# Order of TensorE work in a cross-attention batch: weighing directly behind the second half of the scores, and one wait of the output moved behind the fourth block's first scores

## What is computed

```python
x = x + _L0_xattn_ref(_layernorm(x), ctx_1024, Wq, Wk, Wv, Wp, bp)   # cross attention, 1601 context rows per batch
x = x + _L0_attn_ref(_layernorm(x), ...)                             # self attention over the 64 tokens, with a bias
x = x + _L0_ffn_ref(_layernorm(x), W_fc, W_proj)                     # 512 -> 2048 -> 512, then five spike steps

def _L0_xattn_ref(x, y, Wq, Wk, Wv, Wp, bp):
    q = _split_heads(x @ Wq)
    k = _split_heads(y @ Wk)
    v = _split_heads(y @ Wv)
    attn = jnp.einsum('bhid,bhjd->bhij', q, k) * SCALE
    attn = jax.nn.softmax(attn, axis=-1)
    out = jnp.einsum('bhij,bhjd->bhid', attn, v)
    ...
    return out @ Wp + bp
```

## Time and profile before

| | us |
|---|---|
| three runs | 2047.29, 2052.15, 2051.09 (median 2051.09) |
| the profiled execution, as a whole | 2046.93 |
| its span, first to last instruction | 2045.1 |
| PE busy in the span | 1890.7 (92%) |
| DVE, POOL, ACT busy | 1260.8, 909.0, 867.8 |

### The profile page before, as it was taken

The page is one execution under the profiler, slowest core; times in us unless marked ns, Lnnn a source line. Parts: engine busy times, 40 slices in busy tenths (PEclk is TensorE's granted clock), DMA queues, the critical chain, the costliest instruction groups (busy, mean ns, idle before and its releaser), DMA issues. The chain is left out here.

```text
span 2045.1 us, 65858 instructions
## 1 busy us (share of the span) xinstructions
PE 1890.7 (92%) x28992; PEld 1625.4 (79%) x28992; DVE 1260.8 (62%) x1514; ACT 867.8 (42%) x1078; POOL 909.0 (44%) x856
## 2 busy tenths in 40 slices
PE   6999999999999999999999999999997964699774
PEld 3988888888989888888889898888886853578664
DVE  4466584848475665748484756657474435642888
ACT  3444453545354444535453544445342313234341
POOL 0284453627272644536272726445363013434562
PEclk9999999999999999999999999999999985799887
DMA  5201120202020101201010201011013010222331
GB/s 198 79 4 32 43 72 3 72 3 71 3 72 3 71 29 45 72 3 72 3 71 3 72 3 71 28 47 72 2 64 111 4 32 2 78 73 103 113 123 53
DMA packets 42254, 106.09 MB, mean 52 GB/s; under 512 B 18944, under 2 KB 18944, under 8 KB 41984
## 3 DMA queue, kind: packets, MB, share of 16 engines
q1 hardware_dynamic: 41984, 101.79, 14.0%
HBM read 95.62 MB, written 6.16 MB: 50 GB/s over the span
## 5 line engine op out<-in xcount | busy, mean ns | idle before, releaser
L356 POOL TENSOR_TENSOR fold<-fold,prob 128x256 f32<-128x256 f32 (+1 forms) x704 | 673.1, 956 | 55.2
L76 PE MATMUL ring<-y_parts,wk_s 128*128 128x402 f32 (+1 forms) x3072 | 609.2, 351 | 3.7 <-PEq L129 3.7
L76 PE MATMUL ring<-wv_s,y_parts 128*128 128x512 f32 (+1 forms) x2496 | 598.3, 397 | 0.0
L76 PEld LDWEIGHTS ring<-y_parts,wk_s 128*128 128x128 f32 x3072 | 552.8, 189 | 19.7 <-issue 6.1
L76 PEld LDWEIGHTS ring<-wv_s,y_parts 128*128 128x128 f32 (+1 forms) x2496 | 455.0, 184 | 113.4
L350 POOL TENSOR_TENSOR fold<-prob 128x256 f32<-128x256 f32 x64 | 62.8, 982 | 753.7 <-ACT prob L393 753.7
L370 ACT ACTIVATE k_sb<-ring 128x402 f32<-128x402 f32 (+1 forms) x256 | 129.5, 506 | 376.5 <-PE ring L76 376.5
L506 DVE TENSOR_TENSOR prob<-prob,diag 128x1024 f32<-128x1024 f32 (+1 forms) x192 | 273.6, 1477 | 9.1 <-ACT diag L389 9.1
L383 ACT ACTIVATE prob<-s_ps 128x1536 f32<-128x1536 f32 (+1 forms) x128 | 199.9, 1562 | 142.9 <-PE s_ps L623 142.9
L393 ACT ACTIVATE prob<-prob 128x1024 f32<-128x1024 f32 (+1 forms) x192 | 205.7, 1121 | 1.0 <-DVE prob L506 1.0
L623 PEld LDWEIGHTS s_ps<-q_sb,k_sb 32*64 32x64 f32 x13312 | 157.2, 130 | 40.6 <-issue 39.9
(11 more groups left out here) (143 smaller groups left out, 1709.8 us busy)
## 6 DMA issues: line engine op xcount, KB each, us to landing
y_raw<-yT SPq DMA_DIRECT2D x48, 804.0 KB, 6.1
f_raw<-w_ffn SPq DMA_DIRECT2D x48, 512.0 KB, 3.3
y_raw<-yT SPq DMA_DIRECT2D x16, 792.0 KB, 9.4
p_x<-x SPq DMA_DIRECT2D x2, 1024.0 KB, 6.9
q_scratch<-p_x SPq DMA_DIRECT2D x4, 512.0 KB, 2.6
q_sb<-q_scratch SPq DMA_DIRECT2D x16, 128.0 KB, 6.9
x_sb<-x SPq DMA_DIRECT2D x4, 512.0 KB, 8.3
out<-x_sb SPq DMA_DIRECT2D x8, 256.0 KB, 3.2
```

What stands on the lines that cost most here:

```text
L76: mm = pe.matmul(out, left(a, c), right(b, c), start=(c == 0 and n == 0), stop=(c == DC - 1 and n == 2))
L356: pool.tensor_tensor(acc[0:m], acc[0:m], prob[0:m, i, t, :], ALU.add).then_inc(sum_step, 1)
```

## The change

Two edits in PE's `batch`; nothing else in the program differs.

1. For blocks 1, 2 and 3, `weigh(b - 1, i)` with its wait (`small_output` for block 1, `small_rows` for 2 and 3) moves from behind `keys(b, i, 2)` to ahead of it. It stands directly behind `scores(b, i - 1, 1)` now.
2. The wait for the output of block 3 of the batch before, `small_output(b - 1, 3)` (in batch 0, which has no batch before, `small_rows(b, 1)`), moves from ahead of `scores(b, 3, 0)` to behind it, just ahead of `turn(b, 2)`, the next writer of `small_ps`.

```diff
                 scores(b, 0, 0)
                 keys(b, 1, 1)
                 scores(b, 0, 1)
-                keys(b, 1, 2)
                 if past:
                     small_output(b - 1, 0)
                     weigh(b - 1, 1)
+                keys(b, 1, 2)
                 keys(b, 1, 3)
...
                     spread_peaks(b, i - 2)
                     scores(b, i - 1, 1)
-                    keys(b, i, 2)
                     if past:
                         small_rows(b, i - 2)
                         weigh(b - 1, i)
+                    keys(b, i, 2)
                     keys(b, i, 3)
                 values(b, 0)
+                scores(b, 3, 0)
                 if past:
                     small_output(b - 1, 3)
                 else:
                     small_rows(b, 1)
-                scores(b, 3, 0)
                 turn(b, 2)
```

## The result

| | before | changed |
|---|---|---|
| median | 2050.39 us (6 runs, 2047.29 to 2052.15) | 2130.62 us (6 runs, 2125.41 to 2140.72) |
| ratio | | 1.040, 95% interval 1.037 to 1.043 |
| profiled execution (its span) | 2046.93 us (2045.1) | 2140.72 us (2138.9) |

What follows compares the result with a forecast made beforehand. The prediction took a single chain of PE work to bound the kernel. 9.2 us for the moved weighings plus 5.7 for the output's wait, off 2051.09, gave 2036.2 us, range 2028 to 2046.5.

Steps and rivals of the forecast that it cites:

- supply, in the part on edit 1: Instructions for a weighing right behind scores: arriving every 13.3 ns, needed every 14.2 ns, so no cost, at most 0.06 us.
- the 0.205 us that the seam wins: Per moved weighing, the price of a lone keys unit between small matmuls goes; 45 times, 9.2 us.
- Supply fails outright: Rival, 4%: some 450 instructions in 3.1 us outrun fetching; a 0.33 us stall per place leaves 2051, no change.
- The seam: From scores straight to weighing: 0.15 us from last start to next group, as from scores to keys, so nothing new.
- The output's wait: Ahead of the fourth block's first scores: moving it wins 0.38 us per batch, 5.7 us in 15 batches.
- the 14.9: Both edits together in the cross attention: 9.2 + 5.7 = 14.9 us off the profiled execution.
- The batch length it gave, 92.67 us: One batch of the changed loop: 93.66 - 3 x 0.205 - 0.38 = 92.67 us.
- DVE keeps its time: Condition at the transpose behind the fourth block's first scores: DVE's division ends in time, with 0.9 us to spare.
- I take both as even: POOL's sums 1.7 us later cost DVE's subtraction at most 1 us; POOL's later next sums give it back.
- The clock: Rival, 3%: scores and weighing side by side drop PE's clock to 1.2 GHz; 135 us in 45 places, about 2170.
- the conclusion from the earlier trace: In the cross attention the clock holds at 1.00 with scores and weighing side by side, since nothing is idler than before.
- The case: Evidence against a clock fall: the last four weighings fill only 7.39 of 13.00 us, yet the clock stayed 1.00.

Runs made afterwards that it cites:

- edit 1 alone: Only the three weighings moved, against the kernel before: 2120.88 us, ratio 1.034; with 112 instructions added in the prologue as well, 2058.72 us, ratio 1.005.
- the burst: The kernel before with 1024 small matmuls (4096 PE instructions) added in one unbroken row ahead of batch 0: 2105.68 us, one run.
- after_free112: The changed kernel with 112 unused PE instructions added in the prologue, where PE waits anyway: 2038.47 us, ratio 0.994 against the kernel before.

## Why the prediction was wrong

**What failed: supply, in the part on edit 1.** The step is "I take no cost. As bound ... 0.06 us". I read the two paces inside the scores (34 matmuls in 0.35 us, the rest at 13.3 ns) as the rate at which instructions arrive and compared it with the weighing's 14.2 ns. That compared a pace within a block. What happens when a block is used up in less than 3.5 us, no row of the cross attention before could show, since no 256 instructions were that close there; the 0.06 us was a bound of the queue's head start alone. The cost per moved weighing was 62.6 / 45 = 1.4 us idle with edit 1 alone, seven times the 0.205 us that the seam wins. The rival "Supply fails outright" was the right one by name, with 450 instructions in 3.1 us and fetching as the cause. It got 4%, for "nothing at the scores or weighings of a batch shows such a stall". But nothing could: the lone unit stood between them. Its price was 0.33 us, what would eat the sum and not what a row showed, and it ended at no change. A look at the q8 row, 258 instructions per packet, and a count of the instructions between two units of keys (224 before, 448 after) would have given reason to put it among the likely cases.

**Two rules bear on this step that the prediction did not weigh.** The Trainium skill, "Advanced Engine Details and Errata", section "ISA Cache", gives lines of 16 KB, 256 instructions, and only two of them. The stops 768 instructions apart and the bursts of 128 matmuls agree with the 256, and that the burst ran 251 matmuls, 502 instructions, ahead of its first stop fits the two. The Trainium skill, "Runtime: NRT & Kernel Launch", section "Instruction fetch mechanics", says that crossing such a boundary is mostly hidden, because instructions are issued more slowly than the memory is filled; the trace disagrees: it holds here only where 256 instructions last 3.5 to 4.0 us, and in the burst at full clock each border costs 1.5 to 2.0 us.

**What held.** The seam: the weighing starts 1.39 us behind the scores, as taken, and where no border interferes the keys behind a moved weighing start where the sum put them. The rule of the Trainium skill on the tiling mode ("TensorEngine Tiling (Array Packing)", section "Key Properties") agrees: the new seam is as long as that from scores to keys, 1.39 us from start to start of 112 scores and what follows them, and not free. The output's wait: in the all but stop-free kernel with both edits (`after_free112`), scores begin 847.13 - 844.25 = 2.88 us behind the values, the number worked out from the earlier trace rows. With both, 14.6 us of the 14.9 arrive by the medians and 13.3 by the profiles, once the borders are out of the way. So the sum was about right for both edits together, had instructions been at hand; its two parts were not right for each edit alone. The batch length it gave, 92.67 us, was 0.2 too short: it started from 93.66, but batch 2 before lasts from 235.79 to 329.65, 93.86. The loop of `after_free112` has batches of 92.7 to 93.4.

**What held only by luck: DVE keeps its time.** The prediction took POOL's shift as even and left 0.9 us ahead of the transpose. In `after_free112` (DVE, PE):

```profile
847.84 0.22 DVE L517 TENSOR_TENSOR o_sb<-small_ps,rec 128x64 f32<-128x64 f32 x1
...
848.32 0.44 PE L632 MATMUL small_ps<-ident,fold 128*128 128x128 f32 x2
```

The division ends at 848.06 and the transpose starts at 848.32: 0.26 us to spare, and in one batch PE did wait for it, 0.4 us. The step "I take both as even" was mis-sized by some 0.6 us, and edit 1 alone pays for it. DVE's subtractions show the losing side: 306.1 us in all with both edits, 273.1 with neither at the same borders, while its tree of maxima won back some 18 us.

**The clock** was the rival for the slower side, with 135 us and as a cause of its own. It fell seven times, behind stops, and cost about 12 us of the 94 by which the profiled execution is longer. No program without stops showed a fall between 100 and 1500 us. The neighbourhood of scores and weighing alone does not lower it: in `after_free112` the clock is 1.00 through the batches (windows, PE alone),

```profile
100.00:1535.70 1435.70, 1433.90 (x25035) 1.00 0.11 39
```

so the conclusion from the earlier trace rows was right. The case was not quite as harsh as it looked, though: right behind that stretch, before, PE stood idle and the clock did fall,

```profile
1562.00:1566.40 4.40, 0.00 (x0) 1.00 0.00 0
1566.40:1573.20 6.80, 5.87 (x14) 0.50 0.67 151
```

and whether the thin work or the idle time lowered it, these rows do not part.

**The sum as measured**, for the profiled execution: 79.5 us of stops (66.6 + 12.9), about 12 more where a group restarts with nothing queued (by the starts of the matmuls, 91 us are lost at the stops), 12 of clock, less 14.9, are 88. From the first keys to the first of the last four weighings it is 1496.62 us before and 1585.70 now, 89.1 more. The whole span is 93.8 longer; what is left, nearly 5 us, falls behind the cross attention, in stages that the change does not touch.

## What to carry to other kernels

Count instructions as well as time: where a reordering puts small matmuls side by side, add up the instructions between two stretches of long ones, and if 256 of them last less than the 3.5 to 4.0 us of the burst, price a stop of the difference for each. Work that looks misplaced, like a slow unit between two fast groups, may be what lets the next block arrive. And time a change to such a kernel at more than one alignment, with a few unused instructions ahead of it, before judging it: here the same edits gave anything from 0.6% faster to 4% slower.

## What the runs showed of the hardware that I had not expected

- PE's instructions arrive in blocks of 256, one per 3.5 to 4.0 us in the burst. From a packet's start to PE's restart it took some 2.4 us (261.3 to 263.71), of which the packet itself took 1.
- The place of the borders in a program matters: 40 unused matmuls ahead of an unchanged loop made it 56 us slower, some 4 of them by their own work.
- A border stopped PE in slow work, or for longer, at two places: where the DMA engines were full (2.9 us beside over 300 GB/s), and close behind a loop's jump (up to 2.6 us; none in the one batch that was entered without it).
- Stops of 1 to 2 us among dense work were followed by falls of the clock, but not each: seven falls for 57 stops here, two for 58 with edit 1 alone.
